# A four-layer graph network on one core: one-head sums in three split passes, skip rows added earlier, and an eight-head layer with columns of two heads at once

## The reference

```python
x = layernorm(x + L0(x))   # RGCN: 3 convolutions, 4 relations
x = layernorm(x + L1(x))   # GCN: 2 convolutions
x = layernorm(x + L2(x))   # GAT: 4 heads x 256, then 1 head x 768, with linear skips and norms
x = layernorm(x + L3(x))   # GAT: 8 heads x 96, ELU, then 1 head x 768
# gat_conv
xl = (x @ W).reshape(n, heads, out_ch)
e = leaky_relu(a_src[src] + a_dst[dst], 0.2)
e = exp(e - segment_max(e, dst)[dst])
alpha = e / (segment_sum(e, dst)[dst] + 1e-16)
out = segment_sum(xl[src] * alpha[:, :, None], dst) + bias
```

## Time and profile before

| what | value |
|---|---|
| median of 3 runs | 1421.93 us (1421.38 to 1422.33) |
| the profiled execution | 1422.3 us |
| its span (first to last instruction) | 1420.6 us |
| mean granted PE clock | 0.994 of full |
| PE busy | 1358.8 us, 96% |
| DVE busy | 773.7 us, 54% |
| ACT busy | 446.5 us, 31% |
| POOL busy | 550.3 us, 39% |

### The profile page before, as it was taken

How to read it: one execution, slowest core, us unless ns; L and a number is a source line. 1 busy time by engine, 2 the same in 40 slices (tenths; PEclk the granted TensorE clock), 3 DMA queues, 4 the chain that set the end, 5 groups by cost and what they waited for, 6 DMA issues and landing times.

```text
span 1420.6 us, 22617 instructions
## 1 busy us (share of the span) xinstructions
PE 1358.8 (96%) x7834; PEld 1280.5 (90%) x7834; DVE 773.7 (54%) x1826; ACT 446.5 (31%) x937; POOL 550.3 (39%) x628
## 2 busy tenths in 40 slices
PE   5999999999999999999999999999998999988997
PEld 3676999999999999999999999999887987778897
DVE  6876755223545256465232344657356363589656
ACT  1564522111110000100010132154466333458832
POOL 8000324325234524353424242323345472566830
PEclk9999999999999999999999999999999999999999
DMA  3101111212434133233212131222111320210001
GB/s 118 55 30 35 39 34 44 57 34 86 122 99 124 56 89 108 77 116 102 67 34 62 40 89 34 52 67 81 43 29 50 100 72 12 67 51 1 1 1 55
DMA packets 57803, 86.49 MB, mean 61 GB/s; under 512 B 6467, under 2 KB 54458, under 8 KB 57583
## 3 DMA queue, kind: packets, MB, share of 16 engines
q1 hardware_dynamic: 45204, 65.82, 15.8%
q10 hardware_dynamic: 12504, 19.36, 4.4%
HBM read 83.24 MB, written 1.92 MB: 60 GB/s over the span
## 4 chain that ended last, share of the span: by engine, by line
PE 79%; DVE 10%; ACT 4%; POOL 3%; issue 3%; DMA 1%; DVEq 0%; SPq 0%; ACTq 0%; POOLq 0%
PE psum L2583 13%; PE psum L2586 13%; PE psum L2587 13%; PE psum L2600 8%; PE psum L2603 7%; PE psum L3084 3%; PE psum L2732 2%; DVE max_scratch L2276 2%; PE psum L2657 2%; PE psum L2996 1%; PE psum L2626 1%; PE psum L2629 1%; PE psum L3000 1%; PE psum L3001 1%; PE psum L2572 1%
## 5 line engine op out<-in xcount | busy, mean ns | idle before, releaser
L2583 PE MATMUL psum<-w_lo,xT_hi 128*125 128x384 f32 (+4 forms) x1110 | 378.0, 341 | 3.4 <-POOL w_lo L929 1.6
L2586 PE MATMUL psum<-w_hi,xT_lo 128*125 128x384 f32 (+4 forms) x1110 | 374.0, 337 | 0.0
L2587 PE MATMUL psum<-w_hi,xT_hi 128*125 128x384 f32 (+4 forms) x1110 | 374.0, 337 | 0.0
L916 POOL CAST w_hi<-w_raw 128x384 fp32r<-128x384 f32 x190 | 105.2, 553 | 569.3 <-PE psum L2587 465.9
L1104 ACT ACTIVATE h_hi<-psum 125x384 fp32r<-125x384 f32 (+1 forms) x120 | 59.1, 492 | 529.3 <-PE psum L2587 524.9
L1794 DVE TENSOR_TENSOR h_lo<-psum,h_hi 125x384 fp32r<-125x384 f32 (+1 forms) x120 | 66.9, 558 | 286.7 <-ACT h_hi L1104 285.9
L2583 PEld LDWEIGHTS psum<-w_lo,xT_hi 128*125 128x125 f32 (+1 forms) x1110 | 206.4, 186 | 6.2 <-POOL w_lo L929 3.4
L2586 PEld LDWEIGHTS psum<-w_hi,xT_lo 128*125 128x125 f32 (+1 forms) x1110 | 206.8, 186 | 0.4
L918 POOL TENSOR_TENSOR w_lo<-w_raw,w_hi 128x384 fp32r<-128x384 f32 x190 | 201.2, 1059 | 15.2
L2587 PEld LDWEIGHTS psum<-w_hi,xT_hi 128*125 128x125 f32 (+1 forms) x1110 | 206.6, 186 | 0.0
L2600 PE MATMUL psum<-h_lo,adjacency 125*125 125x384 f32 (+3 forms) x600 | 203.5, 339 | 2.1 <-issue 1.9
(11 more groups left out here) (364 smaller groups left out, 2313.0 us busy)
## 6 DMA issues: line engine op xcount, KB each, us to landing
w_raw<-weights_dram SPq DMA_DIRECT2D x296, 192.0 KB, 2.4
score_w_raw<-weights_dram ACTq DMA_DIRECT2D x58, 192.0 KB, 2.8
x_nat<-x_dram SPq DMA_DIRECT2D x1, 1875.0 KB
x_residual<-x_dram SPq DMA_DIRECT2D x5, 375.0 KB
score_a_rows<-L_gnn_a_src_dram ACTq DMA_DIRECT2D x8, 192.0 KB, 3.4
score_a_rows<-L_gnn_a_dst_dram ACTq DMA_DIRECT2D x8, 192.0 KB, 4.7
out_dram<-x_residual SPq DMA_DIRECT2D x4, 375.0 KB
rgcn_bias<-rgcn_bias_dram SPq DMA_DIRECT2D x1, 1125.0 KB
```

Source lines behind the costliest of these rows:

```text
L916: nc.gpsimd.tensor_copy(mem.wh[:, slot, :], mem.raw[:, raw_slot, :]).then_inc(w_hi_ready, 1)
L2583: ins = nc.tensor.matmul(o, h, wl, start=(j == 0), stop=False, skip_group_check=True)
L2586: nc.tensor.matmul(o, l, wh, start=False, stop=False, skip_group_check=True)
L2587: ins = nc.tensor.matmul(o, h, wh, start=False, stop=stop and j == k - 1, skip_group_check=True)
```

## The change

Q1's sums become three passes of rounded halves, as in Q3: ACT and DVE make a rounded half and a remainder of each of the five attention tiles and of the five feature blocks, and `one_head_part` multiplies them. The features with b2 added go to tiles of their own.

The rows br2, be2 and b2 are all loaded by ACT where b2 alone was. POOL waits for all three ahead of the second piece of Q1, forms the row sum and the first two skip rows, splits up to Q1.chunk + 16, does the other three skip rows, and then splits on.

In Q2 the rows go at blocks 4, 12 and 20 and the columns of head 0 at 21; the last three chunks (not two) run node block by node block. DVE makes the maxima of heads 0 and 1, then columns for both, then the maxima of head 2; head 0's five scores run ahead of its finishes. ACT's split limit ahead of the second piece is one chunk lower, its flat row of head 0 and the first exponentials come between the feature reads. POOL's wait ahead of the casts is on the last Q1 sum. `prob_used` goes with its wait, which only a layer by heads would have taken in `probs`. Left out below are the places of the new tiles in memory, the names of semaphores and the offsets in Q3 that follow from shared ones.

```diff
 PAIR_EVENTS = {3: (("scores", 0),), 6: (("row", 0),), 16: (("send", 0),)}
 LONG_EVENTS = {3: (("scores", 0),), 6: (("row", 0),), 24: (("send", 0),)}
-HEAD_EVENTS = {2: (("scores", 0),), 5: (("row", 0),), 14: (("row", 1),), 23: (("row", 2),), 26: (("send", 0),)}
+HEAD_EVENTS = {2: (("scores", 0),), 4: (("row", 0),), 12: (("row", 1),), 20: (("row", 2),), 21: (("send", 0),)}
 Q0 = Attention(None, HEADS2, C2, KC, PIECES1, True, BASE_L2, True,
 ...
                 nc.gpsimd.tensor_tensor(mem.xres[0:BP, b, :], mem.xres[0:BP, b, :], mem.par[0][0:BP, 0:D], ALU.mult
                                         ).then_inc(gained, 1)
-            split_to(Q1.chunk + 24)
-            pool.wait_ge(params_loaded, 16 * 7)
+            pool.wait_ge(one_head_loaded, 3 * 16)
             nc.gpsimd.tensor_tensor(mem.par[3][0:BP, 0:D], mem.par[3][0:BP, 0:D], mem.par0b[0:BP, :], ALU.add
                                     ).then_inc(rows_added, 1)
             pool.wait_ge(rows_added, 1)
-            for m in range(NB):
+            skip_row(0)
+            skip_row(1)
+            split_to(Q1.chunk + 16)
+            for m in range(2, NB):
                 skip_row(m)
+            split_to(Q1.chunk + 24)
+            pool.wait_ge(params_loaded, 16 * 5)
             split_to(Q1.end)
 ...
             split_to(Q2.end + 8)
             pool.wait_ge(heads_bias_loaded, 16)
-            pool.wait_ge(tile_ready, made_by_vector(Q1, 0, NB - 1))
+            pool.wait_ge(part_done, Q1.unit0 + 2 * NB)
             late_counts = [mem.counts_f[0:BP, 0, :], mem.counts_f[0:BP, 1, :], mem.par0b[0:BP, 0:N]]
 ...
                     ins.then_inc(exp_done, 1)
                 exps_made[q.index] = max(exps_made[q.index], q.turns_within(tiles))
+            def one_prob_hi(k):
+
+                act.wait_ge(tile_ready, made_by_vector(Q1, 0, k))
+                nc.scalar.activation(mem.one_head_prob_hi[k][0:BP, :], source_tile(Q1, 0, k), ACT.Copy
+                                     ).then_inc(prob_hi_ready, 1)
+
+            def one_feat_hi(m):
+
+                act.wait_ge(feat_biased, NB + m + 1)
+                nc.scalar.activation(mem.one_head_hi[0:BP, m, 0:D], mem.biased[m][0:BP, :], ACT.Copy).then_inc(feat_hi_ready, 1)
+
+            def first_exps(k):
+
+                if k < NB - LATE:
+                    source_exp(Q2, 0, k)
+                else:
+                    source_below(0, k)
+                    source_exp_below(0, k)
+
             def feature_product(q, loads={}):
                 n = len(q.pieces)
                 for g, bank_ in enumerate(q.banks[0:NB * n]):
                     piece, m = g // NB, g % NB
                     if m == 0 and piece:
-                        split_hi(q.chunk + (piece + 1) * q.k + 8)
+                        split_hi(q.chunk + (piece + 1) * q.k + (7 if q is Q2 else 8))
+                        if q is Q2:
+                            nc.scalar.activation(mem.elu[0:1, 0, 0, 0:1], mem.ones[0:1, 0:1], ACT.Exp)
+                    if piece and q is Q2 and m >= 2:
+                        first_exps(m - 2)
                     elif g == NB - 1:
 ...
                         else:
                             split_hi(q.chunk + q.k + 8)
-                    elif piece == 1 and q is Q2 and m == 2:
+                    elif piece == 1 and q is Q2 and m == 1:
                         keep_flat(q, 0)
                     elif piece == 1 and q is Q1 and m == 0:
                         keep_flat(q, 0)
                     elif piece == 1 and q is Q1 and m == NB - 1:
-                        for k in range(NB):
-                            source_exp(q, 0, k)
+                        for k in range(NB + 2):
+                            if k < NB:
+                                source_exp(q, 0, k)
+                            if k >= 2:
+                                one_prob_hi(k - 2)
                     if g in loads:
 ...
                     split_hi(Q0.end + AHEAD)
             act.wait_ge(layer_ready, NB)
-            load_part("L2_gnn_b2", par[1], 0, D, b2_loaded)
+            load_part("L2_gnn_br2", par[3], 0, D, one_head_loaded)
+            load_part("L2_gnn_be2", mem.par0b, 0, D, one_head_loaded)
+            load_part("L2_gnn_b2", par[1], 0, D, one_head_loaded)
             split_hi(Q0.end + AHEAD)
-            feature_product(Q1, {NB - 1: ("L2_gnn_br2", par[3], D), NB + 1: ("L2_gnn_be2", mem.par0b, D),
-                                 NB + 3: ("L2_gnn_g2", par[0], D)})
+            feature_product(Q1, {NB + 3: ("L2_gnn_g2", par[0], D)})
             def q1_read(b, half):
 ...
             split_hi(Q1.chunk + 25)
             for i in range(NB + 1):
+                if i == 2:
+                    one_feat_hi(0)
+                    one_feat_hi(1)
+                elif i == 3:
+                    for m in range(2, NB):
+                        one_feat_hi(m)
                 residual_read(Q1, i)
 ...
                     if k == NB - LATE and h >= 2:
                         elu_exp(h - 2)
-            head_exps(0)
+            for k in range(3, NB):
+                first_exps(k)
             for h in range(HEADS3):
 ...
             def scores_begin(q):
-                if q is Q3:
+                if q is Q1:
+                    one = mem.ones[0:BP, 0:2 * NB].rearrange("p (m c) -> p m c", m=NB)
+                    nc.vector.tensor_copy(mem.one_head_hi[0:BP, :, D:D + 1], one[:, :, 0:1])
+                    nc.vector.tensor_tensor(mem.one_head_hi[0:BP, :, D + 1:D + 2], one[:, :, 0:1], one[:, :, 1:2], ALU.subtract)
 ...
             def q1_feature_bias(m):
                 dve.wait_ge(gemm_read, Q1.gemm0 + NB * len(Q1.pieces))
-                f = feat_flat(Q1, m, 0, D)
-                nc.vector.tensor_tensor(f, f, mem.par[1][0:BP, 0:D], ALU.add).then_inc(feat_biased, 1)
+                nc.vector.tensor_tensor(mem.biased[m][0:BP, :], feat_flat(Q1, m, 0, D), mem.par[1][0:BP, 0:D], ALU.add
+                                        ).then_inc(feat_biased, 1)
+
+            def one_feat_lo(m):
+
+                dve.wait_ge(feat_hi_ready, m + 1)
+                nc.vector.tensor_tensor(mem.biased_lo[m][0:BP, :], mem.biased[m][0:BP, :],
+                                        mem.one_head_hi[0:BP, m, 0:D].bitcast(F32), ALU.subtract).then_inc(one_feat_lo_ready, 1)
+
+            def one_prob_lo(k):
+
+                dve.wait_ge(prob_hi_ready, k + 1)
+                nc.vector.tensor_tensor(mem.prob_lo[0:BP, 1 + k, :], source_tile(Q1, 0, k),
+                                        mem.one_head_prob_hi[k][0:BP, :].bitcast(F32), ALU.subtract).then_inc(prob_lo_ready, 1)
             scores_begin(Q0)
 ...
             scores_begin(Q1)
             scores_of(Q1, 0)
-            for step in (score, finish):
-                for k in range(NB):
-                    step(Q1, 0, k)
-            dve.wait_ge(b2_loaded, 16)
-            for m in range(NB):
-                q1_feature_bias(m)
+            for k in range(NB):
+                score(Q1, 0, k)
+            for k in range(NB + 1):
+                if k < NB:
+                    finish(Q1, 0, k)
+                if k:
+                    one_prob_lo(k - 1)
+            dve.wait_ge(one_head_loaded, 3 * 16)
+            for m in range(NB + 1):
+                if m < NB:
+                    q1_feature_bias(m)
+                if m:
+                    one_feat_lo(m - 1)
             for s in range(NB + 2):
 ...
             scores_begin(Q2)
             def head_scores(h):
-                for k in range(NB):
-                    if k == NB - LATE + 1:
-                        if h % 2:
-                            columns(Q2, h + 1, min(h + 3, HEADS3))
-                        for i in range(NB - LATE):
-                            finish(Q2, h, i)
+                at = NB - LATE + 1 if h else NB
+                for k in range(at):
                     score(Q2, h, k)
-
-            scores_of(Q2, 0)
-            scores_of(Q2, 1)
+                if h % 2:
+                    columns(Q2, h + 1, min(h + 3, HEADS3))
+                for k in range(NB - LATE):
+                    finish(Q2, h, k)
+                for k in range(at, NB):
+                    score(Q2, h, k)
+
+            maxima(Q2, 0)
+            maxima(Q2, 1)
+            columns(Q2, 0, 2)
             maxima(Q2, 2)
 ...
                     nc.tensor.transpose(turned_part(q, v, n, n + 1), g_tile(q, j)[:, nodes(c)], mem.ident[0:BP, 0:BP]
                                         ).then_inc(g_turned, 1)
+            def one_head_part(b, u, k):
+
+                if u == 0:
+                    pe.wait_ge(prob_lo_ready, k + 1)
+                    pe.wait_ge(one_feat_lo_ready, k + 1)
+                a, width = Q1.units[u]
+                width += width % 2
+                o = bank(Q1.out_bank(u), 0, width)
+                p_hi, p_lo = mem.one_head_prob_hi[k][0:BP, nodes(b)], mem.prob_lo[0:BP, 1 + k, nodes(b)]
```

(45 more changed lines are left out.)

2 lines of the change are left out of this document (1 added, 1 removed).

## The result

The changed kernel takes 1446.37 us, the median of six runs (1443.26 to 1453.17), against 1421.99 (1421.38 to 1422.33): the ratio is 1.0181, 95% interval 1.0155 to 1.0207. It is slower, as forecast, by 24.4 us where 16.5 were forecast, and 0.4 above the range. The profiled execution took 1443.26 (span 1441.5), the fastest of the six; two more profiles, taken later, took 1451.17 and 1449.75.

A forecast was written before the change was run, and what follows sets the result against it. PE was taken as the bound, with 79% of the chain of waits. Terms 5.4 + 2.6 + 2.8 + 1.5 - 3.5 - 4.45 + 12.3 = +16.65 on 1422.3 gave 1438.9, median 1438.5 us; range 1428 to 1446.

The forecast's parts named there:

- E: Start of Q2: POOL waits for ACT's late w_hi of chunk +19, so z of head 0 comes 12.3 us later.
- R2: Rival: POOL's queue is released before about 1267, so Q2 gains 4.2; 16.5 us less, about 1422; chance 0.10.
- R3: Rival: half clock lasts into Q2's heads, ACT splits one exponential later, or B's gap grows: 1443 to 1450; chance 0.14.
- A: Q1's second piece: POOL waits for three loads and adds skip rows first; PE stands 5.4 us, half clock +2.6.
- R1: Rival: the three loads land together by 1110 to 1112, A falls away; 8.0 us less, 1430.5; chance 0.14.
- B: Q1's attention-weight halves delay the first residual read: PE stands +2.8 us, half clock after it +1.5.
- C: Q1's residual chunks no longer queue behind five skip rows on POOL: -3.5 us.
- D: Q1's sums as three passes, 5.28 us a tile instead of 6.17: -4.45 us for five tiles.
- one execution's distance of 0.4: Last step of the sum: the median of the runs taken as 0.4 us under the profiled execution, 1438.9 to 1438.5.

The follow-up runs named there:

- e1: Changed kernel with POOL's split ahead of the count casts ended one chunk sooner (Q2.end + 7 instead of + 8): 1426.67 us, ratio 1.0044.
- e4: Kernel before with only ACT's split limit ahead of Q2's second piece one chunk lower, as in the changed kernel: 1442.74 us, ratio 1.0155.
- e8: Changed kernel with POOL waiting for two of the three row loads (br2 and be2), b2 on its own semaphore: 1442.60 us.
- e13: Changed kernel with skip rows 2 to 4 on POOL waiting for DVE's one-head columns: 1444.35 us.
- e3: Changed kernel with the edit of e1, and POOL's load wait and five skip rows behind split_to(Q1.chunk + 24): 1420.90 us, ratio 0.9993.
- e7: Kernel before with the three-pass sums alone, skip rows in their old place: 1427.23 us, ratio 1.0036.
- e6: e3 with skip rows between split_to(Q1.chunk + 20) and + 24, and first residual read ahead of the last two prob_hi: 1416.46 us, ratio 0.9961.
- e9: Kernel before with the eight-head part alone and POOL's limit of e1, one-head layer as it was: 1420.16 us, ratio 0.9990.

## Why the prediction was right and wrong

**E was right**, in mechanism and size: POOL held by the w_hi of chunk +19, PE idle 15.4 us (16 said), z 13.7 later against the first maximum (12.8 said). `e1` and `e4` show it from both sides. Both parts came nearly as said: without the hold (`e1`) z comes 3.3 sooner after the first maximum than before (3.95 said), and the hold costs 17.0 (16.8 said). The missing 0.9 is read as the half clock, for which I had taken 0.5 and named 14.5 as the upper end: from the last late product to z are 2.9, where 1.6 were said. In the second and third profile E is 14.9. R2 falls with `e4`, and already with POOL's wait of 23.85 us in the changed kernel. R3's half clock did last into the heads in the second and third profile.

**A failed in size.** The step was: last load at 1115.7, chunk +9 at 1122.3, PE stands 5.4 (from 1117.2 these times give 5.1), and 2.6 of clock; +8.0. The mechanism was as said: loads in turn (R1 falls with `e8`), additions of 1.8, PE waiting for w_lo, then half clock. The stretch measured +11.04 in the first profile, +16.2 and +15.3 in the second and third. In the first, both terms were too small and nothing else came in: PE stood 7.1, and the other 3.9 are the half clock behind it, over my upper end of 3.4; from the columns to the first residual unit are 10.58, and 10.57 in the kernel before (1128.14 to 1138.71). The wait was longer because the loads landed at 1119.2, 2.4 later than I had it once the 1.08 is taken off, for the queue moved 80 and 99 GB/s in the first 6 us, and 132 only then.

In the second and third profile a term comes on top that the sum did not have: PE stands another 3.85 and 2.73 us for DVE's columns, and falls to half clock once more. I priced the skip rows on POOL and PE alone; that three of them now ran beside DVE's columns I did not look at, though the earlier trace rows already show 2.48 for an addition in company and 1.84 for one alone. In `e13`'s one profile this wait is gone, as in the first profile of the changed kernel; why it came in two of three executions stays open.

For DVE beside POOL the Trainium skill has the rule ("SBUF — State Buffer", section "SBUF: two separate sides"): a DVE operation with two SBUF inputs and a GpSimd operation that reads SBUF share a port pair as an exclusive lock, held for the whole instruction. The rows agree that DVE is held up beside POOL's work: 2.45 us for a prob_lo that takes 0.80 alone. That it was held over nine POOL instructions in a row, from within the first to the end of the last, is more than the one instruction that the page tells of.

**B and C** came out at -1.04, not +0.8: PE stood 2.3 for the read (2.8 said), no half clock followed, for which I had taken 1.5, and what is left for C is -3.3 (-3.5 said; no run tests C alone). This error of 1.8 went the other way and hid part of A's. But B's price rests on where the skip rows stand: 2.3 here, 6.0 in `e3`, 10.4 in `e7`. I had put it down to the alternation of ACT and DVE alone.

**D** was right for the tile: 5.28 us, from 1183.19 to 1188.47, as forecast. The sums gave 4.45, and part came back at their end, where PE waited 2.9 for ACT's layer norm (in the kernel before no wait of PE stood within the sums): -3.95 with the earlier rows, not -5.0.

**The median.** I took one execution's distance of 0.4 for all; with gaps that bring the half clock the profiled execution was 3.1 under its own median. Of the 7.9 us between 1438.5 and 1446.37 these two, 3.5 together, are one part, and A's 3.0 in the first profile is another; the rest is 1.1 ahead of the score turn, 1.1 in D and 0.9 in E, less the 1.8 of B and C. The time lies where R3 had it (1443 to 1450, 0.14), but of R3's three reasons only the half clock in the heads shows, and only in two of three profiles.

## What to carry to other kernels

Where a limit of one engine's in-order program is lowered, look up every other engine's program for the count that the old limit made: the next place at which it is made may lie behind a whole stage, and one number then costs 20 to 21 us (`e1`, `e4`). Before work is moved on one engine, list what each other engine does at the new place and whether the two slow each other; here GpSimd additions beside VectorE's two-input operations cost both (2.04 for 1.81 us in `e3` on the one, 2.45 for 0.80 on the other), and the small operation can be the one that starves. A part that loses alone (`e7`, +5 us) and one that loses in its place (A) can win together: `e6`, the change with three edits, is 5.7 us under the kernel before, of which the eight-head part alone (`e9`) gives 1.3.

## What the hardware showed that I had not expected

A 125x5 addition on VectorE took 10.19 us beside back-to-back GpSimd work, 60 times its own 0.17; in another execution of the same kernel the four such operations took 0.82 to 1.76 each. And the clock's fall does not follow from a gap's length alone: PE was idle 1.87 of the 3 us from 1300 in the kernel before (busy times by stretch, first row), with the clock at 1.00 there and behind it, and 1.86 of 3 in `e9` from 1296, with 0.50 behind it (above).

```profile
1300.00:1303.00 3.00, 1.13 (x9) 0.94 (x9) 2.96 (x6) 2.75 (x6) 2.71 (x2) 1.00 0.00 0
1303.00:1306.00 3.00, 3.00 (x30) 3.00 (x30) 2.86 (x9) 2.97 (x8) 2.92 (x3) 1.00 0.02 5
```
